# Filling the spare rows of a sorted table: 32 wide writes during the first half in place of ten early and eight late ones

## What is computed

```python
logits = xt @ gate_w.T
scores = softmax(logits)
top_vals, idx = top_k(scores, 2)
xs = xt[:, None, :] * top_vals[:, :, None]
for e in range(8):
    mask = (idx == e)
    h = silu(einsum('tkd,hd->tkh', xs, w1[e]) + b1[e])
    x2 = einsum('tkh,dh->tkd', h, w2[e]) + b2[e]
    x3 = einsum('tkd,hd->tkh', xs, w3[e]) + b3[e]
    y = y + sum(x2 * x3 * mask[:, :, None], axis=1)
z = silu(xt @ sw1.T) * (xt @ sw2.T) @ sw3.T
out = x + y + z
```

## Time and profile before

| | |
|---|---|
| median of 3 runs | 3453.88 us (3435.41 to 3469.94) |
| the profiled execution | 3477.87 us, span in the trace 3476.0 us |
| PE busy | 2700.4 us (78% of the span) |
| DVE busy | 1862.9 us (54%) |
| ACT busy | 1045.1 us (30%) |
| DMA moved | 155.84 MB in 86279 packets |
| packets on SP's queue (q1) | 73136, 11.1% of 16 engines' span |
| packets on ACT's queue (q10) | 6192, 1.1% |

### The profile page before, as it was taken

One profiled execution on the slowest core, in us unless ns is written; L12 is line 12 of the kernel. 1 busy time (PEld: TensorE's weight loads), 2 busy tenths in 40 slices (PEclk: granted clock), 3 DMA queues, 4 the chain that ended last, 5 costly groups with the idle time before them and its releaser, 6 DMA issues.

```text
span 3476.0 us, 113967 instructions
## 1 busy us (share of the span) xinstructions
PE 2700.4 (78%) x45688; PEld 2098.4 (60%) x45783; DVE 1862.9 (54%) x5000; ACT 1045.1 (30%) x2120; POOL 494.6 (14%) x616
## 2 busy tenths in 40 slices
PE   3788788788788788788788887677777777767883
PEld 3566566566566566566666665566666666655662
DVE  4545555555555555555555555455555555544555
ACT  1333333333333333333333333222222222212221
POOL 2111111111111111111111111111111111111221
PEclk9889999999899999899999998888988898978997
DMA  5011111111111111111111111200000000012225
GB/s 171 22 45 41 31 47 38 31 49 35 37 43 35 37 43 35 37 43 35 37 43 36 37 44 65 96 16 16 16 16 16 16 16 16 16 58 67 69 67 175
DMA packets 86279, 155.84 MB, mean 45 GB/s; under 512 B 11224, under 2 KB 39904, under 8 KB 84576
## 3 DMA queue, kind: packets, MB, share of 16 engines
q1 hardware_dynamic: 73136, 117.78, 11.1%
q0 software_dynamic: 6528, 17.87, 1.4%
q10 hardware_dynamic: 6192, 13.38, 1.1%
HBM read 120.37 MB, written 28.62 MB: 43 GB/s over the span
## 4 chain that ended last, share of the span: by engine, by line
PE 65%; DVE 16%; issue 9%; ACT 5%; DVEq 2%; DMA 2%; SPq 0%; POOL 0%; ACTq 0%; POOLq 0%
PE ps L381 24%; PE ps L715 4%; PE ps L732 4%; PE ps L401 4%; PE ps L569 3%; PE ps L388 3%; PE ps L711 2%; PE ps L1164 2%; PE ps L1479 2%; PE ps L735 2%; PE ps L748 2%; DVE mem L1014 2%; DVE neg_max L1009 1%; ACT mem L788 1%; PE ps L1116 1%
## 5 line engine op out<-in xcount | busy, mean ns | idle before, releaser
L381 PE MATMUL ps<-mem 128*128 128x256 f16 (+1 forms) x4224 | 594.5, 304 | 73.6 <-DVE mem L1348 64.4
L381 PEld LDWEIGHTS ps<-mem 128*128 128x128 f16 x4224 | 458.3, 110 | 190.4 <-DVE mem L1348 68.4
L788 ACT ACTIVATE mem<-ps 128x512 f32<-128x512 f32 (+3 forms) x320 | 177.2, 564 | 456.5 <-PE ps L742 164.3
L381 PE MATMUL ps<-xt,mem 128*128 128x128 f16 x4608 | 281.6, 220 | 30.0 <-DVE xt L1303 30.0
L381 PEld LDWEIGHTS ps<-xt,mem 128*128 128x128 f16 x4608 | 262.5, 98 | 40.7 <-DVE xt L1303 37.7
L463 POOL TENSOR_TENSOR mem<-mem 128x514 f16<-128x514 f32 x136 | 161.2, 1188 | 738.4 <-ACT mem L458 738.4
L1014 DVE RECIPROCAL mem<-ps 128x64 f32<-128x64 f32 x256 | 142.8, 558 | 170.3 <-PE ps L735 165.9
L1030 POOL TENSOR_TENSOR rstd<-var_eps,neg_half 128x1 f32<-128x1 f32 x128 | 70.4, 550 | 1098.2 <-DVE var_eps L889 1098.2
L832 ACT ACTIVATE mem<-ps 128x512 f32<-128x512 f32 x256 | 152.2, 595 | 181.0 <-PE ps L715 181.0
L715 PE MATMUL ps<-mem 64*128 64x128 f32 x2048 | 191.7, 308 | 0.0
L1479 PE MATMUL ps<-mem 128*128 x576 | 157.2, 397 | 32.7 <-ACT mem L1505 32.3
(11 more groups left out here) (256 smaller groups left out, 5221.8 us busy)
## 6 DMA issues: line engine op xcount, KB each, us to landing
mem<-in_ctx_t SPq DMA_DIRECT2D x136, 257.0 KB, 2.7
mem<-in_ctx_n SPq DMA_DIRECT2D x136, 256.0 KB, 3.5
mem<-x_sorted SPq DMA_DIRECT2D x74, 128.5 KB
mem<-y_pairs SPq DMA_DIRECT2D x32, 256.0 KB, 4.0
mem<-in_experts ACTq DMA_DIRECT2D x7, 768.0 KB, 8.6
x<-in_x_tok SPq DMA_DIRECT2D x34, 128.0 KB, 3.3
x_mid<-x SPq DMA_DIRECT2D x32, 128.0 KB, 1.7
x<-x_mid SPq DMA_DIRECT2D x32, 128.0 KB, 2.0
```

Source lines behind the costliest of these rows:

```text
L381: last = pe.matmul(dst, a, b, start=i == 0 and j == 0, stop=i == n - 1 and j == 2)
L788: act.activation(dst, src, ACT.Copy).then_inc(*did(done))
```

## The change

The writes of `spare_row` leave SP. In their place ACT issues one transfer for each tile of the first half, behind the tile's last copy in `scalar2`. Each writes `FILL` = 9 blocks of 128 rows (1152 rows, 1,184,256 bytes) from the same `spare_row`, with the source repeated nine times; the 32 of them cover the whole table, which grows from 35072 to 36864 rows. All 32 count on `spare_in`, and SP waits for them at the end of the join, before `first_over`. The scatters of the second half then write over them. `spare_at`, its copy on DVE, and the eight reads and writes on SP are gone.

```diff
-ROWS = EXPERTS * STRIDE + (EXPERTS + LANES) * P
+FILL = -(-(EXPERTS * STRIDE + (EXPERTS + LANES) * P) // (TILES * P))
+ROWS = TILES * FILL * P
...
-        spare_at = sb("spare_at", [P, EXPERTS], U32)
...
                 act.activation(op_f.rearrange("p c n -> p (c n)"), om4[:, 0].rearrange("p c b q -> p (c b q)"), ACT.Copy, scale=parity[:, 0:1]).then_inc(*did("sel_act"))
+                act.dma_start(sorted_rows[bass.ds(total(t, LANES * FILL * P, lane * FILL * P), FILL * P), :].rearrange("(b p) n -> p b n", p=P),
+                              spare_row[:, :].unsqueeze(1).to_broadcast([P, FILL, ROW])).then_inc(s["spare_in"], 16)
...
-            for e in range(EXPERTS + LANES):
-                sp.dma_start(sorted_rows[EXPERTS * STRIDE + P * e:EXPERTS * STRIDE + P * (e + 1), :], spare_row[:, :]).then_inc(s["spare_in"], 16)
...
             lane_over(1)
+            sp.wait_ge(s["spare_in"], 16 * TILES)
             sp.sem_inc(s["first_over"], 1)
...
             sp.wait_ge(s["planned"], 1)
-            for e in range(EXPERTS):
-                row = sp.value_load(spare_at[0:1, e:e + 1], min_val=0, max_val=ROWS - P)
-                sp.dma_start(sorted_rows[bass.ds(row, P), :], spare_row[:, :]).then_inc(s["spare_in"], 16)
-            sp.wait_ge(s["spare_in"], 16 * (2 * EXPERTS + LANES))
...
-            plan(dve.tensor_copy(spare_at[:, :], next_row[:, :]))
```

## The result

The changed kernel is slower. Over eleven runs of each its median is 3495.36 us (3476.94 to 3508.32) against 3455.94 us (3434.32 to 3470.93): a ratio of 1.0113 with a 95% interval of 1.0083 to 1.0143, that is 29 to 49 us. The forecast was 3443.2 us with a range up to 3482. The profiled execution took 3494.39 us (before: 3477.87).

The account below looks back on a forecast made before the run. PE's work and short DVE and ACT steps bound the first half, SP alone the gap before the third part. -11.04 - 0.20 + 0.5 = -10.7 us, from 3453.9 to 3443.2 us; range 3425 to 3482 us.

Parts of the forecast that it names:

- The end of the second half: Removing SP's eight reads and writes and the `spare_at` copy from the chain gains 11.04 + 0.20 = 11.24 us.
- The issue on ACT: Each new transfer takes 0.8 us to issue (0.79 extrapolated), hidden in ACT's 5.13 us idle gap before `hqt`: cost 0.
- The first rival: The issue on ACT lasts as long as the transfer drains, delaying `hqt` 32 times: 45 us more, 3488 us; chance 0.16.
- the two figures of the forecast: Time one new transfer needs on the DMA engines: 3.2 us at 43 ns a packet, 6.2 us at 192 GB/s.
- The join: At the first half's end, the last transfer delays the weights' load by 0.5 us; later waits cost 0, at worst 2.
- PE's restart: At the third part's start, PE starts about 4 us behind `planned`, its clock stage unchanged: 0.
- the third rival: PE restarts at a higher clock after the shorter idle time before the third part: 3.1 us more gain, 3440 us; chance 0.07.
- Added on the DMA engines: First half: 32 transfers take 100 to 200 us of engines 13% busy; context loads have 27 us to spare: cost 0.
- The second rival: Transfers delay loads, stores or instruction supply: 0.2 us in each of 32 tiles, 4 us in the join, 3453 us; chance 0.16.
- The forecast's own test: The forecast fails if a tile copy on ACT waits behind the issue, or PE's trip grows by more than 0.3 us.

Follow-up runs that it names:

- e4: The changed kernel with its 32 transfers moved to mid-tile, behind the fourth exponential of `scalar2`: 3446.53 us, ratio 0.9949 to the kernel before.
- e1: The changed kernel with the same bytes issued by lane 0's tiles only, as 16 transfers of twice the size: 3456.93 us, ratio 0.9992 to the kernel before.
- e9: The kernel before plus 32 transfers at the tiles' ends, each 128 rows of 9252 bytes copied from weights in DRAM: 3513.71 us, ratio 1.0158 to before.
- e5: The kernel before, small writes kept, plus the change's 32 transfers to rows nobody reads, waited for only at the program's end: 3515.86 us, ratio 1.0179.

## Why the prediction was wrong, point by point

**The end of the second half: right.** 11.24 us were forecast, and the third part is shorter by 11.3 us in the profile, 11.0 in e4. No other wait took the place.

**The issue on ACT: right, and cheaper than taken.** 0.378 us in place of 0.79. The slope from 4 to 128 rows doesn't go on: 1024 more rows cost 0.045 us over the 0.333 us of 128 rows, and e1's 2304 rows took 0.378 us too. The first rival (the issue lasts as long as the drain) is false. The drain lies between the two figures of the forecast, 3.2 and 6.2 us. The landing took 6.4 us in the median, but that runs from the issue; the packets of the transfer at the branch shown are under way for some 4.3 us, from 1167.3 to 1171.6, and in the 2.5 us of the row above 0.73 MB moved, 291 GB/s, not the 192 of the early writes.

**The join: right in outcome.** The weights' landing on the chain is 5.64 us, not longer than the 6.09 us of the earlier trace rows, so the 0.5 us set against it weren't spent. `first_over` and the load of lane 1's tile moved behind the last transfer, as said. The timeline after:

```profile
2228.54 0.51 ACT L862 ACTIVATE mem<-mem,cst 128x256 f32<-128x256 f32 x1 [1.95 <-DVE mem L1017]
...
2237.83 0.33 SPq L1084 DMA_DIRECT2D x<-x_mid  x1
2237.84 3.72 ACTq L1597 DMA_DIRECT2D mem<-in_experts  x7
...
2244.66 1.08 ACT L1249 ACTIVATE mem<-ps 128x512 f16<-128x512 f32 x2 [10.00 <-PE ps L1166]
```

The load is issued 6.8 us ahead of ACT's copy, where it was 11.6 us ahead, and ACT's seven issues end 3.1 us before the copy. The way from L862 to that copy takes 16.1 us, against 16.7 before. The cover was thin and it held.

**PE's restart: right.** Its start is 4.1 us behind SP's first read as forecast, and the third part gained the 11.3 us of the gap and nothing beyond; the third rival has no share.

**The step that failed is "Added on the DMA engines ... Who meets them? ... A delay of even 6 us is hidden: 0".** It looked only for loads that an engine waits for, and found that they have 27 us to spare. It didn't ask what else those engines carry at the places where the transfers run. The profile of before names a queue "instruction", and has PE's branch with 3.5 us, in 14 places where such a transfer would be under way; neither was looked at. The cost set to 0 was 2.8 us of idle time at each of 14 branches (39.4 us) and some 7 us more of busy time at a lower mean clock: 46.4 - 11.3 = 35 us, against 39 us measured (29 to 49).

**The second rival had the right word and the wrong size.** It named "instruction supply" among the things that share the engines, at 0.2 us in each tile. Spread evenly, with the join's 4 us, it came to 10.4 us in its own sum. What happens is all or nothing: 0 at lane 0's end and nearly 3 us at lane 1's, because only there a branch stands behind the transfer. And the argument against it, a DMA load of 13%, is a mean: while a transfer of 1.18 MB runs, the engines are at 103%.

**The forecast's own test** ("PE's time of a trip grows by more than 0.3 us") was the right one: it grew by 3.3 us (46.4/14).

## What to carry to other kernels

Before a large transfer is put into a gap, look at the rows of the loop's line: an engine whose COMPARE_BRANCH takes microseconds, as PE's did here with 3.5 us against 0.05 on the others, may wait there for instructions. Here they came over the same DMA engines as the data, and behind a megabyte of it they arrived some 3 us late, on an engine that has no part in the transfer. The wait may hide in the profile of before under a wait for another engine. Put such a transfer amid the loop's body or behind the branch; smaller pieces ahead of it shortened the delay here, to 0.7 us with nine, but didn't remove it. Where a cost is set to nothing because "DMA is 13% busy", ask who needs the engines in the very stretch in which they are at 100%, the instruction queue among them.

## What the runs showed of the hardware

- PE's branch back to the loop's head took 3.5 us in the median of 14 in the kernel before, at the branch shown with the DMA engines otherwise at rest, while the same branch took 0.05 us on the other engines. At the branch shown a packet of 16 KB on the instruction queue is under way within it, and PE goes on 1.5 us behind its end.
- With transfers of 132 KB (nine in a row), 395 KB (three), 1.18 MB and 2.37 MB ahead of it, PE's branch took 4.3, 4.9, 6.3 and 7.1 us; the packet came 0.1 to 0.6, 1.4 to 1.9, 2.6 to 3.1 and 3.2 to 3.7 us behind PE's last matmul, where it came at once before. The last shows that it isn't held until the transfer's end.
- Eight rows of 9252 bytes for each engine (e9) make PE's branch 6.35 us, 72 rows of 1028 bytes (e5) 6.52 us.
- A DMA of 1152 rows of 1028 bytes is issued in 0.378 us, one of 2304 rows in 0.378 us, and one of 128 rows on SP's queue in 0.333 us.
- 2.4 us more of idle time were followed by a stretch at half the clock (1.2 GHz) that ended about 6.8 us behind PE's restart in place of 5.7 us, at the one branch that I read.
